# Layer 0's opening in an attention and experts kernel: order of the loads, queue of the key stores, place of the output weights

## What is computed

```python
def _L0_xattn_ref(query, key, value, Wq, bq, Wk, bk, Wv, bv, Wo, bo):
    Q = query @ Wq + bq          # query = layernorm(x), key = value = ctx
    K = key @ Wk + bk            # 32 query heads, 8 key heads, head width 16
    V = value @ Wv + bv
    ...
    scores = jnp.einsum('bhgqd,bhkd->bhgqk', Q, K) * scale
    w = jax.nn.softmax(scores, axis=-1)
    y = jnp.einsum('bhgqk,bhkd->bhgqd', w, V)
    y = y.transpose(0, 3, 1, 2, 4).reshape(B, S, EMBED)
    return y @ Wo + bo

x = x + _L0_xattn_ref(_layernorm(x, axis=-1), ctx_4096, ctx_4096, ...)
x = x + _L0_ffn_ref(_layernorm(x, axis=-1), ...)      # 16 experts, 4 per token
x = x + _L1_xattn_ref(_layernorm(x, axis=-1), ctx_4096, ...)
x = x + _L1_ffn_ref(_layernorm(x, axis=-1), ...)
```

## Time and profile before

| | |
|---|---|
| median of 3 runs | 1221.21 us (1220.11 to 1221.81) |
| the profiled execution's own time | 1221.26 us |
| its span, first to last instruction | 1219.9 us |
| granted TensorE clock, mean | 0.993 |
| busy: PE, DVE, ACT, POOL | 97%, 66%, 55%, 34% of the span |

### The profile page before, as it was taken

The page is one execution under the profiler, slowest core; times in us unless marked ns, Lnnn a source line. Parts: engine busy times, 40 slices in busy tenths (PEclk is TensorE's granted clock), DMA queues, the critical chain, the costliest instruction groups (busy, mean ns, idle before and its releaser), DMA issues.

```text
span 1219.9 us, 16555 instructions
## 1 busy us (share of the span) xinstructions
PE 1180.9 (97%) x5936; PEld 912.9 (75%) x5936; DVE 803.5 (66%) x1509; ACT 669.9 (55%) x1561; POOL 420.6 (34%) x517
## 2 busy tenths in 40 slices
PE   8889999999999999899999999999999999999998
PEld 5545556667776777788888888878888888888767
DVE  3467868667776784756666666774456666666877
ACT  2245752577777784355555555653455555556631
POOL 2513534477777772012232232320023223322300
PEclk9899999999999999899999999999999999999999
DMA  8675332785679676321121221121211212211201
GB/s 284 173 166 147 124 117 104 267 233 99 148 198 270 149 145 132 137 70 61 44 67 47 61 70 61 43 79 44 78 44 44 70 61 61 64 49 44 69 1 70
DMA packets 72849, 127.93 MB, mean 105 GB/s; under 512 B 11640, under 2 KB 30968, under 8 KB 70072
## 3 DMA queue, kind: packets, MB, share of 16 engines
q1 hardware_dynamic: 53024, 73.90, 19.9%
q0 software_dynamic: 17296, 48.26, 15.8%
q10 hardware_dynamic: 2448, 4.72, 1.1%
HBM read 150.37 MB, written 26.48 MB: 145 GB/s over the span
## 4 chain that ended last, share of the span: by engine, by line
PE 75%; DVE 6%; POOL 6%; issue 5%; DMA 5%; ACT 3%; SPq 0%; ACTq 0%; POOLq 0%; DVEq 0%
PE bank L466 48%; PE bank L2024 7%; PE bank L1216 6%; PE bank L2000 4%; POOL moe L1599 3%; PE bank L678 2%; POOL xs L1588 2%; PE bank L692 2%; PE bank L644 1%; PE bank L659 1%; DMA moe<-ys,token_out 1%; DMA xs<-xn_rows,token_in 1%; PE bank L1276 1%; PE bank L442 1%; PE bank L2349 1%
## 5 line engine op out<-in xcount | busy, mean ns | idle before, releaser
L1991 POOL TENSOR_SCALAR p<-p,mx 128x256 f32<-128x256 f32 x256 | 163.7, 657 | 505.7 <-DVE mx L1985 505.7
L1183 DVE TENSOR_TENSOR wf_lo<-wf_raw,wf_hi 128x512 fp32r<-128x512 f32 x188 | 121.5, 688 | 34.1 <-ACT wf_hi L1177 31.9
L1977 ACT ACTIVATE p<-bank,mx 128x256 f32<-128x256 f32 x256 | 118.1, 486 | 10.7 <-DVE mx L1967 10.6
L466 PE MATMUL bank<-xnA_hi,w1q_hi 128*128 128x512 f32 x288 | 119.0, 413 | 2.0 <-DVE xnA_lo L460 1.5
L1177 ACT ACTIVATE wf_hi<-wf_raw 128x512 fp32r<-128x512 f32 x192 | 110.2, 626 | 10.0 <-DMA wf_raw<-in_wffn,weight_row 9.9
L466 PE MATMUL bank<-xnA_hi,w1q_lo 128*128 128x512 f32 x288 | 115.0, 399 | 0.0
L466 PE MATMUL bank<-xnA_lo,w1q_hi 128*128 128x512 f32 x288 | 114.6, 398 | 0.0
L1931 ACT ACTIVATE q1T_hi<-bank 128x512 fp32r<-128x512 f32 x64 | 38.3, 598 | 132.7 <-PE bank L466 132.7
L2007 ACT ACTIVATE p1T_hi<-bank 128x512 fp32r<-128x512 f32 x128 | 75.0, 596 | 65.1 <-PE bank L2000 65.1
L1937 DVE TENSOR_TENSOR q1T_lo<-bank,q1T_hi 128x512 fp32r<-128x512 f32 x64 | 44.2, 691 | 93.5 <-ACT q1T_hi L1931 93.3
L466 PE MATMUL bank<-w1o_hi,a1T_hi 128*128 128x512 f32 x256 | 105.2, 411 | 0.2 <-DVE a1T_lo L2035 0.2
(11 more groups left out here) (340 smaller groups left out, 2950.6 us busy)
## 6 DMA issues: line engine op xcount, KB each, us to landing
w_raw<-in_wq SPq DMA_DIRECT2D x64, 256.0 KB, 2.6
w_raw<-in_wo SPq DMA_DIRECT2D x64, 256.0 KB, 2.7
moe<-xn SPq DMA_DIRECT2D x2, 2304.0 KB, 10.9
returned<-moe SPq DMA_DIRECT2D x8, 512.0 KB, 6.6
q0st<-q_rows SPq DMA_DIRECT2D x14, 256.0 KB, 4.7
ctx<-in_ctxT SPq DMA_DIRECT2D x2, 1024.0 KB, 8.6
x<-in_x SPq DMA_DIRECT2D x8, 256.0 KB, 7.8
q_rows<-q0T_hi ACTq DMA_DIRECT2D x8, 256.0 KB
```

The source lines that it names most:

```text
L466: ins = nc.tensor.matmul(ps, a, b, start=(n == 0), stop=(n == len(pairs) - 1))
L1183: nc.vector.tensor_tensor(wf[m % 2][1][:, a, c, :], raw[m % STREAMS][:, a, c, :], wf[m % 2][0][:, a, c, :].bitcast(F32), ALU.subtract).the ...
L1977: ins = nc.scalar.activation(pr1[s % 2][:, h, :], banks.of(("s1", s, n))[:, hh * 2 * P:(hh + 1) * 2 * P], ACT.Exp, bias=m[:, UH + h:UH + h ...
L1991: ins = nc.gpsimd.tensor_scalar(pr1[s % 2][:, h, :], pr1[s % 2][:, h, :], m[:, 3 * UH + h:3 * UH + h + 1], 1.0, ALU.mult, ALU.mult)
```

## The change

Five edits, all in layer 0's attention:

1. SP loads the value weights and their bias behind the x tiles of half 0 and bk, bq, where they stood ahead of them. On PE, values 2 stands ahead of all four `norm_turn` of half 0.
2. The keys of half 0 are stored by SP, behind the x tiles of half 1 and ahead of the context of half 1, after a wait for their remainder; ACT stores them no longer.
3. The output bias and weights are loaded by SP behind `maxima(0)`, ahead of `keys_in(2)`.
4. ACT makes the high parts of the output weights in the unit loop, one at each of i = 0 to 3, behind `softmax_exp`; POOL makes the remainders behind `out_bias(1)`. The waits on `out0_ready` count the two in the new order.
5. Statistics and scaling of half 1 on DVE stand in one run around query block 0, and ACT's square root for them behind its block 0.

```diff
             load(ctxT[0][:, :, :], A["ctxT"][0]).then_inc(S["ld_ctx00"], 16)
-            load(wkv[:, 1], A["wkv0"][:, 1]).then_inc(S["ld_wv0"], 16)
-            load(bv[:, :], A["bv0"].broadcast_to([P, P])).then_inc(S["ld_wv0"], 16)
             for b in range(HB):
                 load(x[:, b, :], A["x"][b]).then_inc(S[f"rows_in{b}"], 16)
             load(bk[:, :], A["bk0"]).then_inc(S["ld_bqk0"], 16)
             load(bq[:, :], A["bq0"]).then_inc(S["ld_bqk0"], 16)
+            load(wkv[:, 1], A["wkv0"][:, 1]).then_inc(S["ld_wv0"], 16)
+            load(bv[:, :], A["bv0"].broadcast_to([P, P])).then_inc(S["ld_wv0"], 16)
             load(wq[:, :, :], A["wq0"]).then_inc(S["ld_wq0"], 16)
...
                 load(x[:, b, :], A["x"][b]).then_inc(S["ld_x_rest"], 16)
+            sp.wait_ge(S["k0_lo"], 1)
+            keys_out(nc.sync, 0)
             load(ctxT[1][:, :, :], A["ctxT"][1]).then_inc(S["ld_ctx01"], 16)
-            load(bo[:, :], A["bo0"].broadcast_to([P, D])).then_inc(S["ld_wbo0"], 16)
-            load(wo_raw[:, :, :], A["wo0"]).then_inc(S["ld_wbo0"], 16)
...
             maxima(0)
+            load(bo[:, :], A["bo0"].broadcast_to([P, D])).then_inc(S["ld_wbo0"], 16)
+            load(wo_raw[:, :, :], A["wo0"]).then_inc(S["ld_wbo0"], 16)
             keys_in(2)
...
-            sp.wait_ge(S["out0_ready"], KT)
+            sp.wait_ge(S["out0_ready"], B + KT)
...
-                pe.wait_ge(S["out0_ready"], KT)
+                pe.wait_ge(S["out0_ready"], B + KT)
...
             values(1, 5)
-            for k in range(2):
-                norm_turn(0, k, k)
             values(2, 6)
-            for k in range(2, HB):
+            for k in range(HB):
                 norm_turn(0, k, k)
             values(3, 7)
...
                 norm_hi(0, k)
-            act.wait_ge(S["k0_lo"], 1)
-            keys_out(nc.scalar, 0)
-            for m in range(2):
+            for m in range(KT):
                 query(0, m)
+                if m == 0:
+                    norm_sqrt(1)
                 act.wait_ge(S["q0_lo"], m + 1)
                 queries_out(nc.scalar, 0, m)
-            norm_sqrt(1)
-            query(0, 2)
-            act.wait_ge(S["q0_lo"], 3)
-            queries_out(nc.scalar, 0, 2)
-            for k in range(KT // 2):
-                out_weight(k)
-            query(0, 3)
-            act.wait_ge(S["q0_lo"], 4)
-            queries_out(nc.scalar, 0, 3)
-            for k in range(KT // 2, KT):
-                out_weight(k)
             for k in range(HB):
                 norm_hi(1, k)
...
                 if 0 <= i + LEAD_T < UNITS0:
                     softmax_exp(i + LEAD_T)
+                if 0 <= i < KT:
+                    out_weight(i)
...
-                dve.wait_ge(S["out0_ready"], KT + b + 1)
+                dve.wait_ge(S["out0_ready"], b + 1)
...
-            for m in range(KT):
+            for k in range(HB):
+                norm_stats(1, k)
+            query(0, 0)
+            norm_recip(1)
+            for k in range(HB):
+                norm_scale(1, k)
+            for m in range(1, KT):
                 query(0, m)
-                if m < 2:
-                    norm_stats(1, 2 * m)
-                    norm_stats(1, 2 * m + 1)
-                if m == 2:
-                    norm_recip(1)
-                    for k in range(HB):
-                        norm_scale(1, k)
...
-            for k in range(KT):
-                pool.wait_ge(S["w0_hi"], k + 1)
-                nc.gpsimd.tensor_tensor(wo[1][:, k, :], wo_raw[:, k, :], wo[0][:, k, :].bitcast(F32),
-                                        ALU.subtract).then_inc(S["out0_ready"], 1)
             pool.wait_ge(S["zeroed"], KRING + 5)
             values_spread(0)
             values_spread(1)
             out_bias(0)
             out_bias(1)
+            for k in range(KT):
+                pool.wait_ge(S["w0_hi"], k + 1)
+                nc.gpsimd.tensor_tensor(wo[1][:, k, :], wo_raw[:, k, :], wo[0][:, k, :].bitcast(F32),
+                                        ALU.subtract).then_inc(S["out0_ready"], 1)
```

## The result

| | before | changed |
|---|---|---|
| median of 6 runs | 1220.66 us (1218.52 to 1222.89) | 1225.06 us (1221.27 to 1227.64) |
| profiled execution | 1221.26, span 1219.9 | 1224.14, span 1222.8 |
| ratio | | 1.0039 [1.0022, 1.0056] |

Slower by 0.4%: 4.8 us on the 1220.66, with the interval from +2.7 to +6.8. The forecast, 1220.5, was wrong, and the range ended at 1223.8. A second timing of the same kernel (experiment e16) gave 1223.83 us, 1.0017 [1.0001, 1.0033]: +0.1 to +4.0 us. The two intervals share +2.7 to +4.0. So the sign is clear, slower where I had forecast faster, and the size is less sure than 4.8 suggests.

What follows compares the result with a forecast made beforehand. PE, busy 97% of the span, was taken as the bound, with time to win only in its waits or half clock. Terms 0.0 - 1.7 + 0 + 1.0 = -0.7 gave a median of 1220.5 us, range 1217.0 to 1223.8.

Steps and rivals of the forecast that it cites:

- Loads of the opening: PE's opening: values 0 to 2 wait for bv, queries still start at 18.49; 0.0 us (bounds -1.7, +2.1).
- ACT's opening: Fourth query block's high part on ACT starts at once, without two output weights ahead of it: -0.4 us.
- Key stores on SP: Fourth query store ahead of the first scores lands sooner without the keys in ACT's ring: -1.7 us, including the 0.4.
- rival D: Query stores of the opening: the ring is no bottleneck, so +0.6 in all, 1221.8 us; chance 0.18.
- Output weights behind the first maxima: SP's ring ahead of batch 2's loads: 1.25 MB more, covered by 4.0 us; 0 (bounds 0, +0.1, with a tail +4).
- rival C: Batch 2's first scores: output weights in the ring push its queries past their use; +4, 1224.5 us; chance 0.15.
- Output weights among the units: Units i = 0 to 3: four weights among ACT's exponentials start the query block later; +1.0 us (bounds +0.3, +2.3).
- POOL behind: POOL's bias and remainders follow the later weight load, until 76, ahead of its first division at 83.58: 0.
- I take a shift won or lost by 90 us as kept to the end: Whole kernel after the opening: PE is the bound there, so a shift by 90 us stays in the final time.
- A: The forecast as summed, with the half clock staying behind the gap before the first scores: 1220.5 us; chance 0.40.
- B: Behind the first scores' gap: the clock holds as the gap shrinks, -2.0, 1218.5 us; chance 0.27.

Runs made afterwards that it cites:

- e16: The changed kernel, unchanged, timed a second time: 1223.83 us, 1.0017 to before.
- e9: Kernel before with only the opening's changes (value weights behind x, key stores on SP, half 1 statistics in one run): 1221.20 us, 1.0005.
- e3: Kernel before with only the output weights moved: loads behind the first maxima, high parts among the units, remainders behind the bias: 1224.10 us, 1.0028.
- e5: Changed kernel with all four output weight parts on ACT at i = 5: 1223.37 us, 1.0017 to before.
- e4: Changed kernel with wo loaded behind the context of half 1 and only bo behind the first maxima: 1222.68 us, 1.0014 to before.
- e2: Changed kernel with bo and wo loaded ahead of the first maxima, behind batch 1's queries: 1222.11 us, 1.0018 to before.
- e1: Changed kernel with bo and wo loaded behind the context of half 1, as before the change: 1224.47 us, 1.0027 to before.
- e8: Kernel before with only the output weights' high parts at i = 0 to 3 and remainders behind the bias, loads still in the opening: 1222.27 us, 1.0014.
- e12: Kernel before with all four output weights' high parts at i = 5, remainders behind the bias, loads still in the opening: 1221.77 us, 1.0001.
- e7: Kernel before with bo and wo loaded ahead of the first maxima and the four weight parts at i = 5, opening otherwise old: 1225.26 us, 1.0033.
- e10: Changed kernel with PE's idle time filled with useless transposes, also ahead of batch 2's first scores: 1224.33 us, 1.0027 to before.
- e11: Kernel before with useless transposes on PE, 16 ahead of the first scores and one behind each of the first seven units: 1222.99 us, 1.0016.
- e17: Kernel before with the gate's and shared expert's loads moved directly behind the maxima of batch 3: 1221.35 us, 1.0009.
- e18: e11 with the gate's and shared expert's loads moved directly behind the maxima of batch 3: 1219.73 us, 0.9990 to before.

## Why the prediction was wrong

- **Loads of the opening, 0.0: right.** bv landed at 12.77 (12.7 forecast), the queries started at 18.40 (18.4).
- **ACT's opening, -0.4: right in size.** The fourth query block's high part came at 32.41 where it was 32.90; the half 1 query block ran at 37.39 with no wait for the normalized tiles.
- **Key stores on SP, -1.7: the sign right, the size and the mechanism wrong.** The fourth block's stores took 40.15 - 33.92 = 6.2 us, not 5.5, and the first scores came 0.95 earlier. The step that failed is "which I read as a queue in the ring": the two columns above show no gain from the keys' ring (5.73 and 5.80 with the keys on ACT, 5.58 to 5.91 on SP, and with the weights in the opening a loss, 7.64 in e9), and the gain in the bytes of bo and wo, which edit 3 takes out of the stores' time. The Trainium skill ("DMA: Bandwidth & Descriptors", section "Issuing engines are not separate DMA queues") had said that transfers interleave on the same engines whoever issues them; the traces agree with it here, 5.73 with the keys' store on ACT (e3) and 5.61 with it on SP (changed). I put this down as rival D and gave it 0.18; its price for the opening (-0.4) was too small, for it left the weights' bytes out.
- **Output weights behind the first maxima, 0: wrong, and the largest miss.** The step that failed is "about half of the 3.2 falls into a slack stretch. I take **0**". The 1.25 MB were counted in bytes at 0.39 MB in a us, as 3.2 us; they held the ring from about 54 to 60. bo moved only 0.10 to 0.16 MB in a us, and what stands behind in the order of the ring did not use the slack. The last load's issue came 1.0 later (forecast 0.9) and its landing 5.2 later on top: 10.44 where it was 5.2. PE also arrived 2 us earlier than before (65.22 against 67.19), so the cover was 4.0 - 2.0; I had taken the 4.0 whole, although the sum itself moved PE ahead by 1.7. 1.0 + 5.2 - 2.0 = 4.2, and the wait is 4.30. This is rival C in place, object and price (+4, 1224.5), to which I gave 0.15 against the row that should have weighed most, the 15.2 us of wo. That the price fits the median as well (1225.06) is in part luck. e3, e5 and e16 show the wait again, and e4, e2 and e1 are without it, which confirms its place; but how much of the loss is its own isn't settled, since these three are still at 1.0014 to 1.0027, and the sorting by clock gives it some 2 us.
- **Output weights among the units, +1.0: right within its bounds, not shown by its path.** e8 has 1.7 (0.1 to 3.4), against e12's 0.1 at i = 5. The forecast was a wait on ACT p that grows by 1; in e8 it grew by 0.4. In the changed kernel it isn't among PE's waits at all: ACT made two of the four weights at 66.73 and 67.73, while PE stood waiting for the load.
- **POOL behind, 0: right.** The remainders ended at 72.12 + 4.95 = 77.1 (76 forecast), and no later work waited for them; POOL's first division, at 87.64, waited for DVE.
- **The clock.** The half clock stayed, as A had it, and B fell. That a wait of 4.3 us would bring a second stretch of it was in no case: the step from marker 1 to 2 took 14.6 us in place of 12.2. Slow steps there occur without the wait too (e8 14.6, e12 14.8, e4 16.2, e7 17.4), so the wait isn't shown to be its cause.
- **"I take a shift won or lost by 90 us as kept to the end": true only roughly.** 4.35 at 180 us became 2.9 in the profiled execution.
- **A slip in the range.** Its upper end, 1223.8, is called C with half its tail, but rival C prices that at 1222.5.

## What to carry to other kernels

Count cover in the ring's time and not in bytes: here a bulk load put ahead of small loads on the same queue delayed the last of them by 6.2 us, about the time that it held the ring, and the slack seen in the stretch of before was of no use to packets behind it. A load moved out of one transfer's way stands in the way of another, so follow every later load of the queue to its first use, with the time at which the bound engine will now arrive there. Time won ahead of a load that comes no sooner can be lost again at that load, as in e10. And look at which execution a trace shows before it is used to explain a median.

## What the runs showed of the hardware that I had not expected

- A DMA issue on SP, 0.43 to 0.49 us in most cases, took 3.12 us at 58.94 in the changed kernel, with the ring at 94% to 123% of the engines' time, and 1.64 us at 88.37 in before, with the ring at 118%. That a full ring holds the issuing queue back fits both; no run isolates it.
- Packets of some 500 bytes kept the ring at 124% with 0.18 MB in a us (62 to 63 in the changed kernel); wo's large ones moved 0.43 MB at 103%; bo, the same row for every partition, 0.12 MB at 47%.
- Filling PE's idle time raised the granted clock (0.991 to 0.994 on average, 0.996 in the profiled execution of e10), and the kernel was not faster for it. In e11 the same left the average where before had it, at 0.993.
- PE stands still for 0.6 to 2.7 us in 18 of the 20 traces, up to some point between 91 and 106 us, where the profile shows nothing that it waits for. In before, in the changed kernel, in e17 and in e18 the ring is then at 109% to 127%; what the pause is stays open.
